# Moving router, token and weight steps in the tail of a float32 decoder layer, and copying the slot indices to a tile of their own

## The reference

```
x = x + attn(layernorm(x))                       # linear attention, 4 heads of 128
x = x + softmax(q k^T / sqrt(512)) v             # q from layernorm(x), k and v from ctx
t = layernorm(x)
x = x + t + mlp(t, shared weights)               # silu(t Wg) * (t Wu) Wd, hidden width 704
      + mixture(t)                               # 16 experts, 2 per token

# mixture: logits = t @ router_w + router_b; probs = softmax; top 2, renormalised
# every (token, choice) pair gets a position in its expert by a running count over
# all tokens, and pairs beyond 640 per expert are dropped; then the expert's mlp
```

## Time and profile before

| | us |
|---|---|
| runs, median of 3 | 1909.42 (1906.35 to 1911.09) |
| the profiled execution's own time | 1909.42 |
| its span | 1907.7 |
| PE busy | 1857.2 (97%) |
| DVE busy | 876.0 (46%) |
| POOL busy | 850.9 (45%) |
| ACT busy | 765.6 (40%) |

### The profile page before, as it was taken

How to read it: one execution, slowest core, us unless ns; L and a number is a source line. 1 busy time by engine, 2 the same in 40 slices (tenths; PEclk the granted TensorE clock), 3 DMA queues, 4 the chain that set the end, 5 groups by cost and what they waited for, 6 DMA issues and landing times.

```text
span 1907.7 us, 27259 instructions
## 1 busy us (share of the span) xinstructions
PE 1857.2 (97%) x10224; PEld 1630.6 (85%) x10224; DVE 876.0 (46%) x2007; ACT 765.6 (40%) x1492; POOL 850.9 (45%) x727
## 2 busy tenths in 40 slices
PE   8999999999999899999999999999999999999997
PEld 5788888888877677777799999999999999999997
DVE  2575557555654444444334444344444344443442
ACT  3444444444453233333244444344444344443331
POOL 2132333233452342222556656566556565566631
PEclk9999999999999899999999999999999999999999
DMA  7002220221253412221576666767666757666632
GB/s 266 18 3 87 89 89 17 73 89 67 78 155 67 77 25 45 44 45 23 114 159 139 140 136 160 150 145 143 131 151 158 148 133 145 132 161 153 139 55 28
DMA packets 208498, 199.18 MB, mean 104 GB/s; under 512 B 132944, under 2 KB 132944, under 8 KB 208112
## 3 DMA queue, kind: packets, MB, share of 16 engines
q1 hardware_dynamic: 183072, 144.34, 28.1%
q0 software_dynamic: 25296, 53.11, 16.5%
HBM read 119.14 MB, written 48.91 MB: 88 GB/s over the span
## 4 chain that ended last, share of the span: by engine, by line
PE 92%; DVE 3%; DMA 1%; ACT 1%; issue 1%; POOL 1%; SPq 1%; ACTq 0%; DVEq 0%; POOLq 0%
PE ps L71 60%; PE ps L1329 21%; PE ps L724 4%; PE ps L730 2%; PE ps L852 2%; PE ps L815 1%; PE ps L741 1%; DVE buffer L1248 0%; DVE buffer L1233 0%; SPq L1038 0%; ACT L1189 0%; ACT buffer L1189 0%; DMA tokens_normed<-buffer 0%; DMA buffer<-in_WkT 0%; POOL buffer L346 0%
## 5 line engine op out<-in xcount | busy, mean ns | idle before, releaser
L71 PE MATMUL ps<-buffer,buffer 128*128 128x320 f32 (+1 forms) x6816 | 1224.4, 340 | 7.1 <-DVE buffer L650 2.1
L71 PEld LDWEIGHTS ps<-buffer,buffer 128*128 128x128 f32 x6816 | 1105.1, 188 | 113.6 <-issue 3.3
L1089 POOL TENSOR_TENSOR buffer<-buffer,buffer 128x512 fp32r<-128x512 f32 x289 | 388.8, 1510 | 268.0 <-ACT buffer L1147 267.7
L1329 PE MATMUL ps<-buffer,buffer 128*128 128x512 f32 x1904 | 446.8, 394 | 21.2 <-DVE buffer L1233 20.7
L1329 PEld LDWEIGHTS ps<-buffer,buffer 128*128 128x128 f32 x1904 | 358.5, 190 | 102.4 <-issue 23.4
L1147 ACT ACTIVATE buffer<-buffer 128x512 fp32r<-128x512 f32 (+4 forms) x689 | 373.9, 595 | 173.4 <-PE ps L1329 90.9
L1248 DVE TENSOR_TENSOR buffer<-ps,buffer 128x320 f32<-128x320 f32 (+1 forms) x240 | 127.6, 532 | 545.5 <-ACT buffer L1189 521.8
L1189 ACT ACTIVATE buffer<-ps 128x320 f32<-128x320 f32 (+1 forms) x240 | 112.4, 468 | 600.1 <-PE ps L71 581.5
L1136 POOL DMA_INDIRECT out_tokens<-buffer,slot_list x80 | 125.9, 1574 | 182.8 <-DVE buffer L1277 177.1
L1233 DVE TENSOR_TENSOR buffer<-buffer,buffer 128x320 fp32r<-128x320 f32 (+1 forms) x240 | 186.5, 777 | 11.1 <-ACT buffer L1147 10.2
L372 POOL DMA_INDIRECT slots<-pairs,slot_u x64 | 67.4, 1053 | 181.8 <-DVE slot_u L711 164.4
(11 more groups left out here) (109 smaller groups left out, 956.3 us busy)
## 6 DMA issues: line engine op xcount, KB each, us to landing
buffer<-in_wts SPq DMA_DIRECT2D x289, 256.0 KB
buffer<-in_x SPq DMA_DIRECT2D x8, 1024.0 KB, 5.8
buffer<-in_ctxT SPq DMA_DIRECT2D x8, 1024.0 KB, 7.7
out_tokens<-buffer SPq DMA_DIRECT2D x8, 1024.0 KB, 4.3
tokens_normed<-buffer SPq DMA_DIRECT2D x32, 256.0 KB, 3.0
out_tokens<-buffer POOLq DMA_DIRECT2D x32, 256.0 KB
tokens_normed<-buffer POOLq DMA_DIRECT2D x1, 1280.0 KB, 8.7
out_tokens<-buffer POOLq DMA_DIRECT2D x1, 1280.0 KB, 12.3
```

The costliest lines, as they stand in the source:

```text
L71: last = pe.matmul(out, left, right, start=(i == 0), stop=(i == len(todo) - 1))
L1089: pool.tensor_tensor(wl[n % RING][:], wraw[n % RAW][:], wh[n % RING][:].bitcast(F32), ALU.subtract).then_inc(s_wl, 1)
L1329: ins = pe.matmul(down_bank[n % 2][:], left, right, start=(c == 0 and i == 0), stop=(c == FC - 1 and i == len(passes) - 1))
```

## The change

Four tables of order change, and one copy is added.

1. At the seam TURN 0 moves on SP from behind WEIGHTS (2, 6) to ahead of WEIGHTS (0, 2); the splits WEIGHTS (6, 8) move from behind SC to ahead of it; TOK 0 moves behind WEIGHTS (8, 16).
2. In `router`, L2 moves to one chunk after L1; the steps of sequences 1 and 2 are placed anew (LP 1 in group 0, TOK 2 behind L2 of sequence 1, X 2 in group 1); TOK of the later sequences moves from chunk 0 to chunk 1.
3. In `scatter_after`, the scatter of sequence b from 2 on moves to chunk 0 of group b.
4. The slot indices are copied from `slot_list` to a tile `slot_index` by DVE in group 7, chunk 1; DVE waits there for the load, and POOL waits for the copy.

```diff
-    ahead = {"V": [("WEIGHTS", (0, 2))], "Q": [("WEIGHTS", (2, 6)), ("TURN", 0)], "SC": [("WEIGHTS", (6, 8))],
-             "PT": [("TOK", 0), ("WEIGHTS", (8, FIRST))]}
+    ahead = {"V": [("TURN", 0), ("WEIGHTS", (0, 2))], "Q": [("WEIGHTS", (2, 6)), ("WEIGHTS", (6, 8))], "PT": [("WEIGHTS", (8, FIRST)), ("TOK", 0)]}
...
-    router = {(0, 0): [("LP", 0)], (0, 1): [("LX", 0), ("L1", 0), ("L2", 0)], (0, 3): [("X", 0), ("TOK", 1)],
-              (1, 0): [("LP", 1), ("TOK", 2)], (1, 1): [("LX", 1), ("L1", 1), ("L2", 1)], (1, 3): [("X", 1), ("LP", 2)],
-              (1, 4): [("LX", 2), ("L1", 2), ("L2", 2)], (2, 0): [("X", 2)]}
-    scatter_after = {(0, 4): 0, (1, 4): 1, (2, 1): 2}
-    for b in range(3, B):
-        router.setdefault((b - 1, 0), []).append(("TOK", b))
-        router[b - 1, 2] = [("LP", b)]
-        router[b - 1, 3] = [("LX", b), ("L1", b), ("L2", b)]
-        router[b - 1, 5] = [("X", b)]
-        scatter_after[b - 1, 5] = b
+    router = {(0, 0): [("LP", 0)], (0, 1): [("LX", 0), ("L1", 0)], (0, 2): [("L2", 0)], (0, 3): [("X", 0), ("TOK", 1)],
+              (0, 5): [("LP", 1)], (1, 0): [("LX", 1), ("L1", 1)], (1, 1): [("L2", 1), ("TOK", 2)],
+              (1, 2): [("X", 1), ("LP", 2)]}
+    scatter_after = {(0, 4): 0, (1, 3): 1}
+    for b in range(2, B):
+        if b >= 3:
+            router[b - 1, 1] = [("TOK", b)]
+            router[b - 1, 2] = [("LP", b)]
+        router[b - 1, 3] = [("LX", b), ("L1", b)]
+        router[b - 1, 4] = [("L2", b)]
         router[b - 1, 5] = [("X", b)]
-        scatter_after[b - 1, 5] = b
+        scatter_after[b, 0] = b
...
-            return bass.IndirectOffsetOnAxis(ap=slot_list[:, e * ET + t, 0:1].bitcast(U32), axis=0)
+            return bass.IndirectOffsetOnAxis(ap=slot_index[:, e * ET + t:e * ET + t + 1], axis=0)
...
-                    pool.wait_ge(s_list, 16)
+                    pool.wait_ge(s_index, 1)
...
+                    if (g, c) == (B - 1, 1):
+                        dve.wait_ge(s_list, 16)
+                        dve.tensor_copy(slot_index[:], slot_list[:, :, 0].bitcast(U32)).then_inc(s_index, 1)
...
-                    if n == tiles_before[B]:
-                        dve.wait_ge(s_list, 16)
```

More of the change, by code:

```diff
@@ L93, in build @@
             "slot_list": sb("slot_list", [P, NSLOT, 2], F32),
+            "slot_index": sb("slot_index", [P, NSLOT], U32),
             "slots": slots,
@@ L872, in phase2 @@
     out = a["out"]
-    slot_list, slots = shared["slot_list"], shared["slots"]
+    ident, slot_list, slot_index, slots = (shared[k] for k in ("ident", "slot_list", "slot_index", "slots"))
     filled, drained = attn["filled"], attn["drained"]
@@ L905, in phase2 @@
     s_down, s_ost = sem("t_down"), sem("t_ost")
-    s_list = sem("t_list")
+    s_list, s_index = sem("t_list"), sem("t_index")
     s_add = [sem(f"t_add{i}") for i in range(ET)]
```

## The result

The changed kernel takes 1959.74 us, the median of 4 runs (1957.38 to 1962.78), beside 1910.03 (1906.35 to 1911.09) for the kernel before: 1.0265 times as long, with a 95% interval of 1.0242 to 1.0287. The profiled execution took 1958.67 us, its span is 1957.0. 1969 was predicted, with a range of 1945 to 1984.

A forecast was written before the change was run, and what follows sets the result against it. PE, busy 97% of the span, was taken as the bound. On 1909.42 us, 7 + 0 + 7 + 21.5 + 8 + 16 = 59.5 gave 1969 us; own range 1957 to 1981, 8-in-10 range 1945 to 1984.

The forecast's parts named there:

- Rival A: Groups 2 to 6: the clock doesn't fall, as 3.2 us of wait is at the edge; 1961 us, chance 0.16.
- The seam, +7: Seam: late loads delay the exponentials and TOK 0, so u2 of group 0 starts late; +7 us, bounds 3.4 and 9.
- Group 0, 0: Group 0: L2 fits in time for X, LP 1 waits about as before; between -3 and +2 us, taken as 0.
- Group 1, +7: Group 1: waits of 12.6 us for 7.02, clock 4.1 for 2.5; +7 us, bounds +1.5 and +10.
- Groups 2 to 6, +21.5 and +8: Groups 2 to 6: waits of 5.6 us for 1.32, +4.3 each, +21.5 in all, with +8 added for the clock.
- 0.9 us for 1.32: Groups 2 to 6, down products: PE's wait for DVE's last low half is 0.9 us, where it was 1.32.
- Group 7, +16: Group 7: late scatter and table load make PE wait 13.6 us for u2's product, clock 2.5; +16, bounds +8 and +19.
- C: Group 7 is cheap, as splits ahead of the scatter or the table's load come sooner: half its cost, 1961 us, chance 0.10.
- B: Groups 2 to 6: `picked` comes in time for X, leaving only TOK's 1.5 us each; 1943 us, chance 0.10.
- D: Not slower: DVE, freed from waiting, gives last low halves in time in groups 1 to 6; 1893 us, chance 0.04.

The follow-up runs named there:

- Run 9: Kernel before with TURN 0 and the splits of chunks 6 and 7 moved as in the change, TOK 0 left ahead of WEIGHTS (8, 16): 1915.11 us.
- run 5: Kernel before with only the steps of sequences 0 to 2 and their scatters placed as in the change: 1913.78 us.
- run 2: Kernel before with only L2 of sequences 3 to 7 moved one chunk later: 1925.78 us.
- run 7: Changed kernel with 13 idle products on PE between u5 and X in groups 2 to 6: 1956.13 us, 1.0247 of before.
- run 8: Kernel before with DVE's chunk 5 part of X behind the last low half and group 1's five splits two chunks earlier: 1899.64 us, 0.9951 of before.
- run 11: Run 8's kernel with the steps of sequences 1 and 2 placed like those of the later ones: 1895.08 us, 0.9919 of before.

## Why the prediction was right, and where its sum was off

**Direction and mechanism: right.** Every new wait that the prediction named, of the probabilities, of LP, of X and of group 7's product, is there, released by what it named. The sum was 10 us too large, and 12 without the 2.17 us at the start, which nobody forecast: that the total came within 9 us is in part luck. Rival A (1961) gave nearly the right time for a wrong reason: the clock did fall in groups 2 to 6.

**The seam, +7, measured +8.33.** Right in its chain: the last exponential was put at 538.2 and began at 540.07, which is 537.9 without the 2.17 us at the start, so that it ended near 538.6; the wait was put at 6.1 and was 6.64. Wrong in the weights. I held TOK 0 to be what decides and put the exponentials alone at 3.4, "half a microsecond" of clock aside. Run 9 shows 7.2 for the exponentials with the clock, 3.4 of it clock, and 1.7 for TOK 0's place. Two misses offset each other: the clock was 3 us too small, TOK's share (3.1) about 1.4 too large.

**Group 0, 0, measured +1.30.** The wait came as put, 2.85 us for 3.03 before, with a slow clock behind it in both. The term left out is LP 1's own work on PE, which moved into this group from group 1; the slow clock took back about 0.5 us of it (an estimate from the lengths of the down products). In group 1 LP 1 took 1.9 us before, from this row to the next product, at 610.18:

```profile
608.31 2.02 PE L724 MATMUL ps<-buffer,rwp 128*32 128x512 f32 x8
```

**Group 1, +7, measured +4.42.** The waits were put at 0.4, 4.0, 6.8 and 1.35 and came as 0.35, 4.00, 7.06 and none: 11.41 us for 7.02, 4.39 more. That this equals the whole difference is chance, as other terms cancel. LP 1's 1.9 us left the group, and X 2's work came into it, 0.5 us by run 5. The clock cost 3.7 us (LP 2 3.62 for 2.02, the unit behind it 6.38 for 5.64, the down products 17.10 for 15.76 at full clock), for 2.5 before: 1.2 more, where 1.6 was put. So the terms that failed are the down wait, which was put at 1.35 and didn't come, and LP 1's work, which was put at nothing and is -1.9. The stretch of L2 by POOL came as put, and is wider than two instructions. POOL, then DVE in group 1:

```profile
655.52 6.28 POOL L1091 TENSOR_TENSOR buffer<-buffer,buffer 128x512 fp32r<-128x512 f32 x5 [38.82 <-ACT buffer L1149]
...
655.91 1.08 DVE L676 TENSOR_TENSOR lg<-lg,linv 128x64 f32<-128x64 f32 x1
...
658.19 1.20 DVE L683 CAST eidx<-topi 128x8 f32<-128x8 uint32 x1
659.42 2.46 DVE L685 TENSOR_TENSOR oh<-iota_e,eidx 128x64 f32<-128x64 f32 x2
```

**Groups 2 to 6, +21.5 and +8, measured +23.05.** LP's wait was put at 1.5 and X's at 3.2; they are 1.40 and 3.07. The failing step is "0.9 us for 1.32" at the down products together with the clock added on top. The two are alternatives, as runs 2 and 7 show: a group that waits 1.12 us there has the clock up, and one with the clock down has no such wait. Per group that leaves 1.40 + 3.07 - 1.32 = 3.15 of waits and about 1.4 of clock (68 down products in 17.15 us, where 68 at the pace of the earlier trace rows, 12.28 for 53, are 15.76). That makes 4.5; measured are 4.6. I had 4.3 + 1.6.

**Group 7, +16, measured +10.14.** The scatter and the load came as put: from POOL's first scatter to the load 11.2 us (968.11 to 979.33), where I had 11.7. The term that failed is the landing: 7.1 us were read from the earlier trace rows, 3.0 came. That row was the very transfer, but with four stores beside it, and in the change these had landed long ago. 4.1 us less make 13.6 into 9.5; the wait was 8.89. The estimate of 2.2 us that the prediction cited from the Trainium skill ("DMA: Bandwidth & Descriptors", "Anatomy of one DMA — SWDGE (gpsimd) path") was the nearer one, for a transfer without company, though that section is about transfers issued by GpSimd and this one goes out on SyncE; no run with the stores beside it came under 6.9. The clock behind the wait cost 1.5 us (36 products in 9.93 for 8.45) against 2.5 put, and the group's later waits changed little (3.05 and smaller ones, where the kernel before has 3.67).

**Rivals.** C had half of group 7's cost gone; 6 of the 16 us were, but neither the splits nor the load came sooner, only the landing. B and D fell: each of the five waits of X is 3.06 or 3.07. D's thought, that DVE's order sets the down wait, was sound, but its lever is X behind the last low half (runs 8 and 11), not L2.

## What to carry to other kernels

A wait taken from one step of an in-order engine's program is not a gain if the step moves towards its consumer: price the move by the gap between producer and consumer in the timeline, and use spare time early, as runs 8 and 11 do. A slow clock behind a wait counts in full where PE is the last to arrive (the seam) and almost nothing where another engine arrives later (groups 2 to 6), so compare it with the next wait instead of adding it. A step that moves takes its own work along, as LP 1 did with 1.9 us from group 1 to group 0: price the work in both places, not only the wait. And a transfer's landing time belongs to its company: ask what is in flight beside it now, and what after the change.

## What the runs showed of the hardware

**POOL holds DVE for longer than one instruction.** At the seam four copies of 16-bit elements took 5.86 us beside POOL's eight subtractions, and 1.46 in run 9, where POOL was idle. In group 7 one subtraction on DVE took 6.26 us (elsewhere 0.68) beside six of POOL in a row:

```profile
990.08 7.47 POOL L1091 TENSOR_TENSOR buffer<-buffer,buffer 128x512 fp32r<-128x512 f32 x6
...
991.85 6.26 DVE L1235 TENSOR_TENSOR buffer<-buffer,buffer 128x512 fp32r<-128x512 f32 x1
```

One of POOL's takes 7.47 / 6 = 1.25 us, so DVE lost to several in a row. The Trainium skill's page "SBUF — State Buffer", in its section "Who interferes with whom", says that copies and casts in their modes with two ports compete with GpSimd for a shared port pair, which the one that issues first keeps for its whole instruction, and that an operation with two inputs in SBUF competes with GpSimd's reads. The kinds held here agree, though no row shows in which mode the copies ran; that a run of instructions keeps DVE out is more than the page states.

**The same wait did not always lower the clock.** In run 2 X's five waits of 3.06 us were followed by the lower level in three groups and not in two, in one execution of equal groups. At the seam of the kernels that leave it alone the first wait of 2.04 us did it in four runs and not in three; a window behind it in the kernel before and in run 2:

```profile
534.12:538.16 4.04, 1.96 (x16) 1.73 (x17) 2.48 (x4) 2.93 (x6) 2.51 (x2) 1.00 1.06 196
534.74:538.15 3.41, 3.41 (x16) 3.18 (x16) 1.39 (x3) 2.78 (x5) 2.50 (x2) 0.52 1.07 182
```

So the prediction's premise that 2.04 us cost no clock held in its own trace only. With the idle time filled, in run 7, the clock stayed up five times of five. The Trainium skill's page "TensorE: Matmul & The Clock Gate" has idle time lower the clock, and run 7 agrees. That page, in "Part 1: The HAM clock gate (the "warmup" mystery)", calls the number of slow products at a kernel's start variable from run to run; of waits like these it doesn't say so, and what chose among the equal ones here stays open.

**A load's landing** of 2.9 to 3.0 us alone became 6.9 to 9.1 with four stores of 256 KB from POOL's queue beside it.
